# Graph network of four layers on one core: the first attention's source rows gathered into a ring, its segments found by comparison, and message rows loaded one turn earlier

## The reference

```python
def _gat_layer(x, src, dst, W, a_s, a_d, b, heads, outc):
    h = (x @ W).reshape(N, heads, outc)
    alpha_s, alpha_d = (h * a_s).sum(-1), (h * a_d).sum(-1)
    e = leaky_relu(alpha_s[src] + alpha_d[dst], SLOPE)
    p = exp(e - segment_max(e, dst)[dst])
    alpha = p / (segment_sum(p, dst)[dst] + 1e-16)
    return segment_sum(h[src] * alpha[:, :, None], dst).reshape(N, heads * outc) + b
# layer 0: two attentions (3 heads, then 1), each with selu, and a product
# layer 1: m = silu(einsum(x[col], edge_attr, W_msg)) @ W_lin, summed by source row, then an update of the nodes
# layer 2: reflections from both ends of each edge, summed by source and by destination
# layer 3: edge matrix (edge_attr @ kernel + bias) times x[dst], summed by source
```

## Time and profile before

| what | us |
|---|---|
| median of 3 runs | 26084.06 (26073.52 to 26091.56) |
| the profiled execution, own time | 26059.39 |
| its span in the trace | 26057.3 |
| POOL busy | 18368.4 (70% of the span) |
| DVE busy | 16265.3 (62%) |
| PE busy | 15985.8 (61%) |
| first attention, from its block's start to the end of its block | 3961.8 |

### The profile page before, as it was taken

One profiled execution on the slowest core, in us unless ns is written; L12 is line 12 of the kernel. 1 busy time (PEld: TensorE's weight loads), 2 busy tenths in 40 slices (PEclk: granted clock), 3 DMA queues, 4 the chain that ended last, 5 costly groups with the idle time before them and its releaser, 6 DMA issues. The chain is left out here.

```text
span 26057.3 us, 352712 instructions
## 1 busy us (share of the span) xinstructions
PE 15985.8 (61%) x99055; PEld 11771.6 (45%) x99058; DVE 16265.3 (62%) x41454; ACT 3861.1 (15%) x8407; POOL 18368.4 (70%) x17570
## 2 busy tenths in 40 slices
PE   4200000026666663888884588888888838999993
PEld 3200000015555552666663355554554526777772
DVE  9466666617777771777774366666666654666664
ACT  0000000012222221111110111111111101222220
POOL 0477777767777774777773577777777767888884
PEclk6555555555555555888885688888888967889886
DMA  3111111101111110111112011111111120000002
GB/s 125 48 33 32 33 33 32 32 13 32 31 32 32 31 30 9 25 25 25 25 26 66 16 19 20 20 19 20 20 19 20 20 71 22 25 24 25 25 25 73
DMA packets 1032548, 815.57 MB, mean 31 GB/s; under 512 B 602135, under 2 KB 922911, under 8 KB 1028513
## 3 DMA queue, kind: packets, MB, share of 16 engines
q0 software_dynamic: 561792, 189.30, 5.8%
q1 hardware_dynamic: 366264, 291.81, 4.2%
q10 hardware_dynamic: 104400, 333.49, 3.2%
HBM read 416.39 MB, written 396.80 MB: 31 GB/s over the span
## 5 line engine op out<-in xcount | busy, mean ns | idle before, releaser
L891 POOL DMA_INDIRECT gat_got<-table,gat_idx x6250 | 5951.9, 952 | 1907.4 <-issue 1903.6
L1389 POOL DMA_INDIRECT msgs<-msg_msg,msg_pos x4875 | 5815.2, 1193 | 1550.0 <-issue 1484.7
L1624 POOL DMA_INDIRECT sheaf_got<-table,sheaf_idx x3125 | 3181.5, 1018 | 952.6 <-issue 952.6
L1288 PE MATMUL msg_dps<-msg_dhotq,msg_dleft 128*128 x16500 | 3437.8, 370 | 0.0
L1288 PE MATMUL sheaf_dps<-sheaf_dhotq,sheaf_dleft 128*128 x18000 | 3335.3, 342 | 0.8 <-DVE sheaf_dhotq L1271 0.8
L353 PE MATMUL hist_s_counts<-hist_s_hot_k,hist_s_hot_a 128*98 128x128 bf16 x3125 | 362.8, 314 | 3567.0 <-DVE hist_s_hot_k L306 3567.0
L1197 PE MATMUL place_look_ps<-place_nexts,place_hot_at 98*128 98x128 f32 x5000 | 1635.7, 467 | 1320.9 <-DVE place_same L1102 924.4
L1288 PEld LDWEIGHTS msg_dps<-msg_dhotq,msg_dleft 128*128 x16500 | 1814.8, 114 | 1346.1 <-issue 570.0
L1288 PEld LDWEIGHTS sheaf_dps<-sheaf_dhotq,sheaf_dleft 128*128 x18000 | 1818.9, 102 | 1305.2 <-issue 252.6
L1498 ACT COPY msg_flip<-msg_fps 128x384 f32<-128x384 f32 (+1 forms) x3000 | 1361.7, 494 | 5383.6 <-PE msg_fps L1456 5374.0
L1632 POOL DMA_INDIRECT msgs<-sheaf_msg,sheaf_pos x1625 | 1786.2, 1099 | 519.2 <-issue 519.2
(11 more groups left out here) (468 smaller groups left out, 27861.8 us busy)
## 6 DMA issues: line engine op xcount, KB each, us to landing
gat_got<-table,gat_idx POOLq DMA_INDIRECT x6250
msg_ex<-ex SPq DMA_DIRECT2D x250, 400.0 KB
gat_sums<-gat_acc ACTq DMA_DIRECT2D x125, 675.0 KB, 3.3
msgs<-msg_msg,msg_pos POOLq DMA_INDIRECT x4875
tail_m<-msgs SPq DMA_DIRECT2D x75, 800.0 KB
src_sums<-tail_acc ACTq DMA_DIRECT2D x75, 800.0 KB
gat_sums<-gat_acc ACTq DMA_DIRECT2D x125, 425.0 KB, 2.6
ex<-zeros ACTq DMA_DIRECT2D x25, 2000.0 KB
```

The lines of the kernel that those rows point to most:

```text
L891: pool.indirect_dma_start(got[b][:, j, :], None, table, bass.IndirectOffsetOnAxis(idx[b][:, j:j + 1], 0)).then_inc(gathered[b], 16)
L1288: last = pe.matmul(self.acc[:, n, 0:self.BQ], left, hot_q, start=False, stop=False, skip_group_check=True)
L1389: pool.indirect_dma_start(msgs, bass.IndirectOffsetOnAxis(pos[b][:, j:j + 1], 0), msg[b][:, j, :], None).then_inc(scattered[b], 16)
L1624: pool.indirect_dma_start(got[b][:, j, :], None, table3, bass.IndirectOffsetOnAxis(idx[b][:, j:j + 1], 0)).then_inc(gathered[b], 16)
```

## The change

Five things are done. **One:** the rows of `table1` are made before the count ("att1" without its scatters; the start rows are scattered later, in a block `put1` of 128 indirect transfers behind the search for segments), and all source indices are loaded at once (`src_all`, 1.6 MB). **Two:** POOL gathers the first AHEAD = 32 chunks' rows, 800 indirect transfers, into `ring` (32 chunks of 25 x 20 numbers a partition) inside the block of the count. **Three:** in the first attention POOL gathers only the chunks 32 to 124, each into the place of the chunk 32 before it as soon as DVE is done with that; the indices come from `src_all`, and POOL's code is written out instead of looped. **Four:** the segments by destination are found by comparing each edge's destination with the one before it; the marks' 128 scatters, their load and their table go, and one indirect gather fetches each partition's first segment. **Five:** in both messages stages SP loads `att` and `ex` of chunk i+1 before it waits for the scatters of chunk i-2.

```diff
+AHEAD = 32
...
-    marks = {o: dram(f"marks_{o}", [P * cols_of[o], 2]) for o in ("d", "s")}
+    marks = {"s": dram("marks_s", [P * C_S, 2])}
+    segment_rows = dram("segment_rows", [NR, 2])
...
-        def count_destinations(zeros):
+        def count_destinations(zeros, table, src_all, ring):
...
+                @block.gpsimd
+                def _(pool):
+                    for i in range(AHEAD):
+                        for j in range(CW):
+                            c = i * CW + j
+                            pool.indirect_dma_start(ring[:, i, j, :], None, table,
+                                                    bass.IndirectOffsetOnAxis(src_all[:, c:c + 1], 0)).then_inc(ahead_got, 16)
+                    pool.wait_ge(ahead_got, 16 * CW * AHEAD)
...
-                    parts = ((ex32, EXW, C), (ex4, 4, C), (marks["d"], 2, C), (marks["s"], 2, C_S), (msgs, D, C_S),
+                    parts = ((ex32, EXW, C), (ex4, 4, C), (marks["s"], 2, C_S), (msgs, D, C_S),
                              (msgs_2, D, C_S))
...
+        def find_segments_by_destination():
...
+                dst_all, ahead = sb("dst_all", [P, C], I32, ctx), sb("dst_ahead", [P, 1], I32, ctx)
...
+                @block.vector
+                def _(dve):
+                    ch = Chain(dve, steps)
+                    dve.memset(ahead[:, :], -1).then_inc(cleared, 1)
+                    ch.link(dve.memset(zero[:, :], 0.0))
+                    dve.tensor_tensor_scan(incl[:, :], cnt[:, :], zero[:, :], 0.0, ALU.add, ALU.add).then_inc(totals, 1)
...
+                    ch.link(dve.tensor_tensor(g["start"][:, :], end[:, :], cnt[:, :], ALU.subtract))
+                    ch.add(dve.tensor_scalar(mark[:, :, 0], g["start"][:, :], 1.0, None, ALU.add))
+                    dve.tensor_copy(mark[:, :, 1], end[:, :]).then_inc(marked, 1)
...
+                    dve.wait_ge(came, 32)
+                    ch.add(dve.tensor_tensor(keep["d"][:, 1:C], dst_all[:, 1:C], dst_all[:, 0:C - 1], ALU.is_equal))
+                    ch.link(dve.tensor_tensor(keep["d"][:, 0:1], dst_all[:, 0:1], ahead[:, :], ALU.is_equal))
+                    ch.add(dve.tensor_scalar(fresh[:, :], keep["d"][:, :], BIG, -BIG, ALU.mult, ALU.add))
+                    dve.wait_ge(looked, 16)
+                    a1, b = seg[:, 0:1], seg[:, 1:2]
...
+                    ch.link(dve.tensor_copy(g["fix_put"][:, :], v[:, 7:8]))
+
+                @block.tensor
+                def _(pe):
+                    pe.wait_ge(totals, 1)
+                    pe.matmul(ps[0:NP, 0:1], earlier[0:NP, 0:NP], incl[:, NK - 1:NK], start=True, stop=True
+                              ).then_inc(offs, 1)
+
+                @block.sync
+                def _(sp):
+                    sp.dma_start(dst_all[:, :], dst_v).then_inc(came, 16)
+                    sp.wait_ge(cleared, 1)
+                    with nc.allow_non_contiguous_dma(reason="one edge a partition"):
+                        sp.dma_start(ahead[1:P, :], dst_v[0:P - 1, C - 1:C]).then_inc(came, 16)
+                    sp.wait_ge(marked, 1)
+                    sp.dma_start(node_rows(segment_rows), mark[:, :, :]).then_inc(kept, 16)
+
+                @block.gpsimd
+                def _(pool):
+                    pool.wait_ge(came, 32)
+                    pool.wait_ge(kept, 16)
+                    pool.indirect_dma_start(seg[:, :], None, segment_rows, bass.IndirectOffsetOnAxis(dst_all[:, 0:1], 0)
+                                            ).then_inc(looked, 16)
...
-                    if o == "d":
-                        ch.add(dve.tensor_scalar(fresh[:, :], mk[:, :, 1], 0.0, -BIG, ALU.is_gt, ALU.mult))
...
-        def attention(name, heads, feats, table, tw, sums, last_rows, extra):
+        def attention(name, heads, feats, table, tw, sums, last_rows, extra, src_all=None, ring=None):
...
-                idx = [sb(f"{name}_idx{b}", [P, CW], I32, ctx) for b in range(2)]
-                got = [sb(f"{name}_got{b}", [P, CW, tw], F32, ctx) for b in range(2)]
+                if ring is None:
+                    idx = [sb(f"{name}_idx{b}", [P, CW], I32, ctx) for b in range(2)]
+                    got = [sb(f"{name}_got{b}", [P, CW, tw], F32, ctx) for b in range(2)]
...
-                        if not first:
-                            sp.wait_ge(gathered[b], 16 * CW * turn)
-                        sp.dma_start(idx[b][:, :], src_v[:, bass.ds(i * CW, CW)]).then_inc(idx_in[b], 16)
+                        if ring is None:
+                            if not first:
+                                sp.wait_ge(gathered[b], 16 * CW * turn)
+                            sp.dma_start(idx[b][:, :], src_v[:, bass.ds(i * CW, CW)]).then_inc(idx_in[b], 16)
...
-                    run_turns(pool, NCH, body)
+
+                    def follow(i):
+                        pool.wait_ge(done, i - AHEAD + 1)
+                        if i >= AHEAD + 2:
+                            pool.wait_ge(gathered[i % 2], 16 * CW * (i // 2 - AHEAD // 2))
+                        pool.sem_inc(admitted, 1)
+                        for j in range(CW):
+                            c = i * CW + j
+                            pool.indirect_dma_start(ring[:, i % AHEAD, j, :], None, table,
+                                                    bass.IndirectOffsetOnAxis(src_all[:, c:c + 1], 0)
+                                                    ).then_inc(gathered[i % 2], 16)
+                    if ring is None:
+                        run_turns(pool, NCH, body)
+                    else:
+                        for i in range(AHEAD, NCH):
+                            follow(i)
...
-                    def ask(i, b, turn, first):
+                    def rows(i, b):
+                        if ring is None:
+                            return got[b][:, :, :]
+                        return ring[:, bass.ds(i % AHEAD, 1), :, :].rearrange("p o t w -> p (o t) w")
+
+                    def ask(i, b, turn, first, stashed=False):
...
-                        dve.wait_ge(gathered[b], 16 * CW * (turn + 1))
-                        g_a = got[b][:, :, feats:feats + heads].rearrange("p t f -> p f t")
+                        if ring is None:
+                            dve.wait_ge(gathered[b], 16 * CW * (turn + 1))
+                        elif not stashed:
+                            dve.wait_ge(gathered[b], 16 * CW * (turn + 1 - AHEAD // 2))
+                        g_a = rows(i, b)[:, :, feats:feats + heads].rearrange("p t f -> p f t")
...
-                        g_x = got[b][:, :, 0:feats].rearrange("p t f -> p f t")
+                        g_x = rows(i, b)[:, :, 0:feats].rearrange("p t f -> p f t")
...
-                    run_turns_woven(dve, NCH, lambda now, before: extra.vector(dve, now, before, ask, weigh))
+                    def turn_of(i, b, turn, first, stashed):
+                        extra.count(dve, i, b, turn, first)
+                        ask(i, b, turn, first, stashed)
+                        weigh(i, b, turn, first)
+
+                    if ring is None:
+                        run_turns_woven(dve, NCH, lambda now, before: extra.vector(dve, now, before, ask, weigh))
+                    else:
+                        turn_of(0, 0, 0, True, True)
+                        turn_of(1, 1, 0, True, True)
+                        with dve.Fori(1, AHEAD // 2) as k:
+                            turn_of(2 * k, 0, k, False, True)
+                            turn_of(2 * k + 1, 1, k, False, True)
+                        with dve.Fori(AHEAD // 2, NCH // 2) as k:
+                            turn_of(2 * k, 0, k, False, False)
+                            turn_of(2 * k + 1, 1, k, False, False)
+                        turn_of(NCH - 1, 0, NCH // 2, False, False)
...
-            def vector(self, dve, now, before, ask, weigh):
-                if now:
-                    self.hist.dve(dve, *now)
-                    ask(*now)
-                    weigh(*now)
+            def count(self, dve, i, b, turn, first):
+                self.hist.dve(dve, i, b, turn, first)
...
                 @block.sync
                 def _(sp):
-                    def body(i, b, turn, first):
+                    def rows(i, b, turn, first):
                         if not first:
                             sp.wait_ge(outered, 2 * i - 2)
                         sp.dma_start(att[b][:, :, :], attr_v[:, bass.ds(i * CW, CW), :]).then_inc(att_in[b], 16)
                         sp.dma_start(ex[b][:, :, :], ex_v[:, bass.ds(i * CW, CW), :]).then_inc(ex_in[b], 16)
+
+                    def places(i, b, turn, first):
                         if not first:
                             sp.wait_ge(scattered[b], 16 * cp * turn)
                             sp.sem_inc(let_in, 1)
                         sp.dma_start(pos[b][:, :], pos_rows[:, bass.ds(i * CP, cp)]).then_inc(pos_in[b], 16)
                         sums.load(sp, i, b, first)
-                    run_turns(sp, NCH, body)
...
```

(26 more changed lines are left out.)

45 lines of the change are left out of this document (38 added, 7 removed).

## The result

The changed kernel takes 25137.2 us (median of 4 runs, 25105.2 to 25141.9) where the kernel before took 26078.8 beside it (4 runs, 26070.7 to 26091.6): a ratio of 0.9636, 95% interval 0.9619 to 0.9653. That is 942 us less, against 891 forecast; 25193 was forecast and the range 25020 to 25350 holds the result. The profiled execution took 25105.15 us, its span 25103.4.

A forecast was written before the change was run, and what follows sets the result against it. POOL was taken to bound the first attention and messages stages, DVE the count. Terms +205 - 179 + 110 - 977 - 50 = -891 us gave 25168 from the profiled execution, forecast as a 25193 us median, range 25020 to 25350.

The forecast's parts named there:

- The count, +205 forecast: Count with 800 gathers beside it: 1000 us of gathers, 2 for landing, 25 for the fill, 1027 for 822 us.
- The 25 us put down to the zero fill: Count: allowance for gathers slowed by the zero fill, 25 us taken between bounds of nothing and 88 us.
- one of my own signs of being wrong: Count: the prediction called itself wrong if the gathers there had gaps beyond 0.3 us.
- The search, -179 forecast: Search for segments: comparison, `fresh`, smaller loads and one gather take 16 us for 195; bounds 12 and 30.
- The split of att1, +110 forecast: Layer 1 rows in two parts: 124 us, then 168 us of scatters, together 292 for 182 us.
- The first attention, -977 forecast: First attention: 93 chunks of gathers at 31.5 us, plus 24 and 10 us, 2985 for 3962 us.
- the 10 us that I added for slower ones beside scans: First attention: 10 us added because DVE's scans, stretching a gather from 0.94 to 0.99 us, fill more time.
- the 23.7 at which it would take over: First attention, rival that DVE becomes the bound: decides from 23.7 us a turn; at 25 us, 160 more; chance 0.07.
- The messages stages, -50 forecast: Both messages stages: POOL's scatters bound them, the wait on `ex` is slack; shifted products shorten the mean scatter, -50 us.
- one product in each turn would begin some 0.2 us into one: 0.3 to 0.4 us less for 125 turns: Second messages stage: a product freed by a landing starts earlier within a scatter than the 0.54 us seen before.
- The slower rival: Count: the 800 gathers stall behind the zero fill, slower overall beyond a 2.46 us pitch; 26405 at 2.8 us; chance 0.03.
- the rival before: Written-out gathers issue slower: a gap after every 128, 24 x 2.8 = 68 us, giving 25260; chance 0.05.

The follow-up runs named there:

- The slowed turn: Changed kernel with an idle memset of 4000 columns at the start of each DVE turn of the first attention: 25326.1 us (one run).

## Why the prediction was right

**What bounds each stage** was read rightly, and by the step that mattered: the count is DVE's and POOL is free in it, the first attention is POOL's, and the messages stages' waits on `ex` are slack. The expected gain came from moving 800 gathers, and the kernel with 16 chunks, 322 us slower, shows that this is what pays; the one with 26 shows how far.

**The count, +205 forecast, +207 found** (1029 for 822). The size was right, in part by luck: one of its three terms had the wrong cause. The pitch of 0.94 + 0.30 us is there, and the 2 us for landing. The 25 us put down to the zero fill are not the fill's: nearly twice the fill left the gathers and the gaps as they were. They are the seven gaps in an unbroken row of transfers, 30 us, which vanish with a wait for landings in each chunk. Gaps beyond 0.3 us in the count were one of my own signs of being wrong, and this sign came. The same kind of gap stood in the row on which I rested a rival (3.14 us before the last of 128 scatters). I laid it to written-out code and set it aside as a thing of a block's end. It was neither. That it comes at the 113th in the count and at the 128th in the series of 128 stays open. Nor did I foresee that the count itself would slow down beside the gathers, from 822 to 846 us; POOL's longer work hides it.

**The search, -179 forecast.** The new block lasts about 16 us, and bringing the old one back costs 179 us. **The split of att1, +110 forecast:** 124 and 168 us, as worked out. No part of it was tried by itself.

**The first attention, -977 forecast, -990 found.** The gathers keep 954 ns; the 10 us that I added for slower ones beside scans did not come, since 3125 of them had 956 before. DVE falls back on POOL at chunk 96 and not 92: it needs 21.4 us a turn, not 21.0, which changes the place and not the end. The slowed turn shows that DVE is the next bound, here at 25.3 us a turn; the 23.7 at which it would take over is worked out and not measured.

**The messages stages, -50 forecast, -84 found** (-99 and +15; by undoing the order, 100 and -23). The mechanism was right and the size off. The step that was mis-sized is "one product in each turn would begin some 0.2 us into one: 0.3 to 0.4 us less for 125 turns". The second half's product does begin there (0.09) and brings 0.28 us a chunk, close to that. The first half's, which I left where it was, now begins at 1.24 us instead of 0.89, just behind the point from which the next scatter slips through, and brings 0.50 us more. Together that is 0.80 us a chunk instead of 0.4. In the first stage I expected little; the same order moved the first product the wrong way, from 0.55 to 0.89, where its scatters are stretched by 1.24 us a chunk instead of 1.07. The start of 0.54 us that I took from the earlier trace rows was that of one product; over the stage it was 0.89 (median), and the second half's product mostly did not begin beside an unhindered scatter at all. By the inference in the Trainium skill ("SBUF — State Buffer", Who interferes with whom), that a `tensor_tensor` leaves descriptor making alone, this term would be 0. The runs speak against it: a product that reads both its inputs from SBUF and was begun 0.64 us later in a scatter lengthened the next one by 0.57. The rule on GpSimd's reads, which the prediction took from the same section, may still hold: a scatter's places lie in an SBUF tile (`msg_pos`), and their reading could be what is held up. No run separates the two.

**The slower rival** (gathers behind the fill) fell with the doubled fill: the pitch stays at 1.25 us where 2.46 would have been needed. The Trainium skill's rule in "DMA: Bandwidth & Descriptors" (Queues, rings and completion order), that each DMA engine goes round its queues a packet at a time, agrees with this as far as a pitch on POOL can show it. In that rival's text 1.36 us is a pitch; the mean gather of that series took 1.03 us. And 24 x 2.8 in the rival before is 67, not 68. Neither changes anything.

Left over are about 17 us less in stretches that the change does not touch (-11, -4, -2). Between two profiles of the changed kernel the same stretches differ by 19 us, so most of this can't be told from the spread. One part is steady: five of the kernel's six series of 128 gathers have a mean of 969 to 971 ns before and 951 to 954 in every profile of a changed kernel, some 2.3 us for each series. Why is open, and so is whether the kernel or the chip makes it, as the kernel before has one profile only.

## What to carry to other kernels

Where one engine bounds one stage and stands idle in another, look first for data that the bounded stage needs and the idle one could fetch, and stop at the point where the idle stage is full: 26 chunks brought as much as 32. A long wait of an engine that is not the stage's bound is worth nothing by itself. But where one engine's instruction holds up another's, as a DVE product does POOL's scatter here, the moment at which the wait ends matters: it brought 0.8 us a chunk in one stage and cost 0.2 in the other, so try both orders in each stage. A row of more than 100 indirect transfers without a wait for landings deserves a look at its idle times.

## What the runs showed of the hardware that was not expected

**Gaps in long rows of indirect transfers.** POOL stops for 3.1 to 7.3 us after every 113 indirect gathers (128 rows each) when it issues them without a wait: 7 times in the 800 of the changed kernel, 3 in 400, 5 in 650. With a wait for the transfers of two chunks back before every 25, there were none in 800 or in 2325, and 28 us of idle time went, of which 7 came back as a longer pause at the block's end. A gap of 3.1 to 5.0 us also stands before the last of each series of 128 scatters, even where POOL waits for DVE's rows in between, and one of 3.2 to 3.5 us before the last of the 128 gathers of L692. The 128 gathers of L536, with waits for landed rows, have none.

**What a DVE product costs a scatter.** A scatter that is held up by DVE's product ends some 0.8 us after the product. Its cost rises with the product's start within the pitch of 1.27 us, and drops by a whole pitch where the product begins from 1.23 us on.

**Which DVE instructions hold POOL up.** Not every long one does. Beside the one-hot instruction of 3.48 us (L308), which reads one operand from PSUM (the tile of numbers `aside`) and one from SBUF, the gathers keep 0.94 us. Beside the product L1555, with both in SBUF, a scatter of 0.97 takes 3 to 4.3. The one gather of the search took 4.20 us beside the comparison, whose operands both lie in SBUF (3.42 us), and `fresh` behind it; which of these two held it to the end is not separated. That the operands' place is what tells the two kinds apart agrees with the Trainium skill ("SBUF — State Buffer", Who interferes with whom), by which an instruction with at most one SBUF input, outside the two-port modes, does not contend with GpSimd. No run here changed the place alone, and the two kinds differ in more: the one stands beside gathers, the other beside scatters.
